# Layer 0 of a two-layer recurrent block: seven smaller place steps on VectorE, the scores one step later, and the rotation of x and the weights at the last gate product

## The reference, cut to what matters

```python
xn = layernorm(x)
s  = attention(xn)          # layer 0: linear attention, 16 heads of 8; layer 1: another linear form
g  = silu(ffn(xn))          # layer 0: 8 experts of width 352, top 2; layer 1: 160 experts of width 64, top 8
x  = x + s * g
```

```python
probs = sigmoid(x @ router_w.T + expert_bias)
top_w, top_idx = top_k(probs, 8)
top_w = top_w / (top_w.sum(-1) + 1e-9) * 2.5
combine[t, top_idx] = top_w
routed = einsum(silu(einsum(x, w_gate)) * combine, w_down)
```

## Time and profile before

| | before |
|---|---|
| median of 3 runs | 1617.26 us (1605.86 to 1618.96) |
| the profiled execution | 1617.64 us, of which the span from first to last instruction is 1615.5 us |
| PE busy | 1270.6 us, 79% of the span |
| DVE busy | 889.2 us, 55% |
| ACT busy | 553.5 us, 34% |
| POOL busy | 553.7 us, 34% |
| mean granted TensorE clock | 0.875 |

### The profile page before, as it was taken

The page is one execution under the profiler, slowest core; times in us unless marked ns, Lnnn a source line. Parts: engine busy times, 40 slices in busy tenths (PEclk is TensorE's granted clock), DMA queues, the critical chain, the costliest instruction groups (busy, mean ns, idle before and its releaser), DMA issues. The chain is left out here.

```text
span 1615.5 us, 20441 instructions
## 1 busy us (share of the span) xinstructions
PE 1270.6 (79%) x6336; PEld 704.5 (44%) x6336; DVE 889.2 (55%) x2575; ACT 553.5 (34%) x1170; POOL 553.7 (34%) x574
## 2 busy tenths in 40 slices
PE   3699988988888898889799891179978777877762
PEld 2334333333333333333333331056966656776652
DVE  3345575675665664665765757600054685486561
ACT  1232322322312322312322220157856355545620
POOL 0000043042052052052061162600065666656565
PEclk9589998998998987998999995579989988898975
DMA  8920020210210210210210213168744444444331
GB/s 270 338 98 1 25 80 27 69 41 22 79 36 17 79 36 17 79 34 18 72 41 12 79 46 119 46 219 255 223 134 121 131 137 131 136 132 138 97 90 42
DMA packets 123235, 152.07 MB, mean 94 GB/s; under 512 B 15277, under 2 KB 82413, under 8 KB 122374
## 3 DMA queue, kind: packets, MB, share of 16 engines
q1 hardware_dynamic: 106758, 117.36, 22.5%
q0 software_dynamic: 16384, 33.59, 7.4%
HBM read 73.30 MB, written 77.60 MB: 93 GB/s over the span
## 5 line engine op out<-in xcount | busy, mean ns | idle before, releaser
L1097 POOL DMA_INDIRECT y<-y_rows,idxy x256 | 269.5, 1053 | 283.7 <-DMA y_rows<-ys 136.8
L1064 POOL DMA_INDIRECT rows<-xn,idx x256 | 252.1, 985 | 83.9 <-issue 82.2
L935 ACT ACTIVATE hs<-GY 128x512 f32<-128x512 f32 x176 | 105.3, 598 | 377.6 <-PE GY L695 306.6
L711 PE MATMUL ACC<-hs,wff 128*128 128x512 f32 x352 | 200.7, 661 | 0.0
L695 PE MATMUL GY<-xn0T,wff 128*128 128x512 f32 x352 | 189.2, 620 | 0.0
L1038 POOL TENSOR_TENSOR rs<-rs,neg_half 128x4 f32<-128x4 f32 x16 | 16.4, 1024 | 453.1 <-DVE rs L1135 453.1
L701 PE MATMUL B<-xw,wff 128*128 128x512 f32 (+2 forms) x272 | 122.6, 630 | 40.9 <-DVE hs L1428 40.9
L1500 DVE SCALAR_TENSOR_TENSOR pos<-neg,pos 128x1024 f32<-128x1024 f32 x8 | 9.8, 1231 | 262.3 <-issue 192.3
L1428 DVE TENSOR_TENSOR hs<-hs,B 128x512 f32<-128x512 f32 x96 | 65.8, 686 | 128.6 <-PE B L701 65.7
L1242 DVE TENSOR_TENSOR att<-X,causal 128x512 f32<-128x512 f32 x128 | 82.6, 686 | 87.7 <-PE X L583 50.7
L842 PE MATMUL X<-y,ident 128*128 128x128 f32 x480 | 78.0, 329 | 64.1 <-DVE y L1587 60.5
(11 more groups left out here) (274 smaller groups left out, 2180.7 us busy)
## 6 DMA issues: line engine op xcount, KB each, us to landing
xg<-rows SPq DMA_DIRECT2D x104, 256.0 KB
y_rows<-ys SPq DMA_DIRECT2D x104, 256.0 KB
rows<-zero SPq DMA_DIRECT2D x7, 2048.0 KB, 9.5
rows<-zero SPq DMA_DIRECT2D x1, 12288.0 KB, 53.9
wff<-in_wgz SPq DMA_DIRECT2D x2, 3840.0 KB, 38.4
wd<-in_wd SPq DMA_DIRECT2D x1, 5120.0 KB, 24.8
wff<-in_w SPq DMA_DIRECT2D x3, 1408.0 KB, 9.2
rows<-xn,idx POOLq DMA_INDIRECT x256
```

Source lines behind the costliest of these rows:

```text
L711: nc.tensor.matmul(ACC[:, :], w2_0[:, v, :], hs[:, v % RH, :], start=(v == 0), stop=(v == U0 - 1))\
L935: nc.scalar.activation(hs[:, u % RH, :], G[u % 2][:, :], ACT.Silu).then_inc(sem["silu_ready"], 1)
L1064: pool.indirect_dma_start(rows, bass.IndirectOffsetOnAxis(ap=idx[:, t * 8 + k:t * 8 + k + 1], axis=0), xn1[:, t, :], None)\
L1097: pool.indirect_dma_start(y8[:, i % RG, k, :], None, y_d[0:groups * Q * P, :], bass.IndirectOffsetOnAxis(ap=idxy[:, b, t * 8 + k:t * 8 + k ...
```

## The change

The table `STEPS` is rewritten. The three reciprocal instructions of `topk1b` become a step of their own, `topk1c`, in slot 20, after `exp0`. The place work is cut into `place_a` to `place_f`, in slots 22, 25, 27, 31, 35 and 39, and `table` in slot 44, where before it was three steps in slots 23, 25 and 28. Scatter goes from slot 29 to 40, qkv0 and rope from 30 and 31 (+2t) to 32 and 33, kp, cum, outer, den and states two or three slots later. qk_T goes from 43 + 10t to 45 + 10t, the scores from 46 and 48 to 49 and 51, the masks from 47 and 49 to 50 and 52, av from 51 to 54; cw0_T, oT_copy, wo and s0 two or three slots later. No instruction is added or removed but for waits. The wait for `acc_done` ahead of the rotation's two copies is taken out.

```diff
@@ -136,16 +136,17 @@
 
 STEPS = {0: ["res_silu"], 1: ["res_gate"], 3: ["res_T"], 4: ["res_add"], 6: ["res_norm"], 9: ["xn1_T", "res_r1"],
          10: ["xn1T_copy"], 11: ["norm0a"], 12: ["router1"], 13: ["probs1"], 14: ["norm0b"], 15: ["topk1a"],
-         16: ["xn0_T"], 17: ["xn0T_copy"], 18: ["topk1b", "router0"], 19: ["exp0"], 21: ["rank"], 48: ["topk0a"], 61: ["topk0b"],
-         23: ["place_a"], 25: ["place_b"], 28: ["place_c"], 29: ["scatter"], 38: ["kp"], 39: ["cum", "outer"], 40: ["den_a"],
-         41: ["states", "den_b"], 72: ["cw0_T", "cw0T_copy"], 82: ["oT_copy"], 84: ["wo"], 85: ["s0"]}
+         16: ["xn0_T"], 17: ["xn0T_copy"], 18: ["topk1b", "router0"], 19: ["exp0"], 20: ["topk1c"], 21: ["rank"],
+         22: ["place_a"], 25: ["place_b"], 27: ["place_c"], 31: ["place_d"], 35: ["place_e"], 39: ["place_f"], 40: ["scatter", "kp"],
+         41: ["cum", "outer"], 42: ["den_a"], 43: ["states", "den_b"], 44: ["table"], 50: ["topk0a"], 62: ["topk0b"],
+         75: ["cw0_T", "cw0T_copy"], 85: ["oT_copy"], 86: ["wo"], 87: ["s0"]}
 for t in range(T):
-    for at, name in ((30 + 2 * t, "qkv0"), (31 + 2 * t, "rope"), (43 + 10 * t, "qk_T"), (44 + 10 * t, "qkT_copy"),
-                     (46 + 10 * t, "scores_a"), (47 + 10 * t, "mask_a"), (48 + 10 * t, "scores_b"), (49 + 10 * t, "mask_b"),
-                     (51 + 10 * t, "av"), (45 + 10 * t, "weights_a"), (50 + 10 * t, "weights_b")):
+    for at, name in ((32 + 2 * t, "qkv0"), (33 + 2 * t, "rope"), (45 + 10 * t, "qk_T"), (46 + 10 * t, "qkT_copy"),
+                     (49 + 10 * t, "scores_a"), (50 + 10 * t, "mask_a"), (51 + 10 * t, "scores_b"), (52 + 10 * t, "mask_b"),
+                     (54 + 10 * t, "av"), (47 + 10 * t, "weights_a"), (54 + 10 * t, "weights_b")):
         STEPS.setdefault(at, []).append((name, t))
 RES = {"res_silu", "res_gate", "res_T", "res_add", "res_norm", "res_r1", "xn1_T", "xn1T_copy", "router1", "probs1",
-       "topk1a", "topk1b", "rank", "place_a", "place_b", "place_c", "weights_a", "weights_b", "scatter"}
+       "topk1a", "topk1b", "topk1c", "rank", "place_a", "place_b", "place_c", "place_d", "place_e", "place_f", "table", "weights_a", "weights_b", "scatter"}
 
 GZ = E1 // 2 * 3 * INTER
 
@@ -1300,6 +1301,9 @@
                 link(nc.vector.tensor_reduce(s8[:], m8[:], AX.X, ALU.add))
                 join()
                 nc.vector.tensor_tensor(chosen, pr2, pr, ALU.not_equal).then_inc(sem["chosen_ready"], 1)
+
+            def s_topk1c(t):
+                join()
                 link(nc.vector.tensor_scalar(s8[:], s8[:], 1e-9, None, ALU.add))
                 join()
                 link(nc.vector.reciprocal(s8[:], s8[:]))
@@ -1318,6 +1322,8 @@
                 link(nc.vector.tensor_scalar(pagesi[:], pagesi[:], 7, None, ALU.arith_shift_right))
                 join()
                 link(nc.vector.tensor_copy(pagesn[:], pagesi[:]))
+
+            def s_place_b(t):
                 join()
                 link(nc.vector.tensor_tensor(new[:], pagesn[:], pages[:], ALU.subtract))
                 link(nc.vector.tensor_copy(hj[:, 0:1], given[:, E1 - 1:E1]))
@@ -1330,21 +1336,27 @@
                 join()
                 link(nc.vector.tensor_tensor(dshift[:], shift[:], shiftn[:], ALU.subtract))
                 link(nc.vector.scalar_tensor_tensor(base[:], shiftn[:], float(P), run[:], ALU.mult, ALU.add))
-                join()
-
-            def s_place_b(t):
-
+
+            def s_place_c(t):
+
+                join()
                 link(nc.vector.scalar_tensor_tensor(shift[:], new[:], 0.0, dshift[:], ALU.is_equal, ALU.mult))
                 link(nc.vector.tensor_scalar(scr[:], dshift[:], float(P), None, ALU.mult))
                 for i, bank in enumerate((X0, X1)):
                     link(nc.vector.tensor_tensor(pr2[:, 2 * i:2 * i + 2, :], bank[:, 0:2 * E1].rearrange("p (t e) -> p t e", t=2),
                                                  limit[:].unsqueeze(1).broadcast_to([P, 2, E1]), ALU.is_le))
+
+            def s_place_d(t):
+
                 join()
                 link(nc.vector.tensor_tensor(shift[:], shift[:], shiftn[:], ALU.add))
                 link(nc.vector.tensor_tensor(pr2, pr2, scr[:].unsqueeze(1).broadcast_to([P, T, E1]), ALU.mult))
                 for i, (bank, done_) in enumerate(((X0, "ranka_read"), (X1, "rankb_read"))):
                     nc.vector.tensor_tensor(place[:, 2 * i:2 * i + 2, :], bank[:, 0:2 * E1].rearrange("p (t e) -> p t e", t=2),
                                             base[:].unsqueeze(1).broadcast_to([P, 2, E1]), ALU.add).then_inc(sem[done_], 1)
+
+            def s_place_e(t):
+
                 dve.wait_ge(*seen.next("ranka_read"))
                 dve.wait_ge(*seen.next("rankb_read"))
                 join()
@@ -1355,7 +1367,7 @@
                 dve.wait_ge(*seen.next("chosen_ready"))
                 nc.vector.tensor_tensor(place, place, chosen, ALU.mult).then_inc(sem["places_ready"], 1)
 
-            def s_place_c(t):
+            def s_place_f(t):
                 dve.wait_ge(*seen.next("places_ready"))
                 nc.vector.memset(pause[:], 0.0)
                 for t in range(T):
@@ -1372,6 +1384,8 @@
                 nc.vector.scalar_tensor_tensor(idx[:], pos_q[:], 1.0 - P, pos_r[:], ALU.mult, ALU.add).then_inc(sem["idx_ready"], 1)
                 link(nc.vector.scalar_tensor_tensor(idxy[:, batch[0], :], pos_q[:], 1.0 - P, pos_r[:], ALU.mult, ALU.add))
 
+            def s_table(t):
+                join()
                 for k in range(JB):
                     link(nc.vector.tensor_scalar(scr[:], given[:], jcol[:, k:k + 1], 0.0, ALU.is_le, ALU.add, accum_out=cj[:, k:k + 1]))
                     join()
@@ -1409,7 +1423,6 @@
 
                     dve.wait_ge(*seen.next("xn0T_ready"))
                     dve.wait_ge(*seen.next("cw0T_ready"))
-                    settled(dve, seen, "acc_done")
                     link(nc.vector.tensor_copy(cw0T[:], cw0Tn[:]))
                     nc.vector.tensor_copy(xn0T[:], xn0Tn[:]).then_inc(sem["rot_ready"], 1)
                 def scaled(e):
```

## The result

| | before | after |
|---|---|---|
| median of 17 runs, same chip | 1610.5 us (1594.94 to 1620.94) | 1597.2 us (1586.94 to 1606.33) |
| ratio, 95% interval | | 0.994 [0.9912, 0.9968] |
| profiled execution / its span | 1617.64 / 1615.5 us | 1586.94 / 1584.8 us |
| mean granted TensorE clock | 0.875 | 0.896 |

The change brought 10 to 13 us where 28 were forecast. The time is inside the range and in the class "within 1%" (0.22), not in the likeliest one. The two profiled executions are 31 us apart and the medians 13: before's lies near the top of what its 17 runs took, after's is the shortest of its 17. So the traces show well which wait went where, and poorly what the sum is worth.

What follows compares the result with a forecast made beforehand. Stage 1 was taken as bound by PE's queue, its idle time and half clock. Terms -25 + 10 - 1.6 - 7.5 - 9.6 - 8 + 14 = -28 took 1617.64 to 1590 us, range 1562 to 1609.

Steps and rivals of the forecast that it cites:

- within 1%: Outcome class for the whole kernel: time within 1%, 16 us, of the kernel before; chance 0.22.
- Part 1: Place work split: PE's wait before unit 7's up product shrinks, new waits come; -25 us in six batches, clock +10.
- Part 2: Last batch with units, f0(7): idx and scatter come later, final res_norm waits for the scatter; only -1.6 us arrive.
- Part 3: Rotation at each batch's start: copies run during down products, PE's waits vanish; -7.5 us (0 to -7.5).
- Part 4: Scores one slot later: PE's wait for ACT's qm shrinks from 4.92 to 3.3 us; -9.6 us, half clock -8.
- Part 5: New slots put topk0b ahead of the second tile's mask_b: av waits 1.4 us, third tile 0.6; +14 us in seven batches.
- I assume this stall stays: Before the second tile's scores: ACT's late silu 13, after 11.35 us idle that no queue ends, was taken as unchanged.
- Rival B: Little arrives: clock falls in all six batches, Part 4 gives nothing, sum 0; with half of Part 4 about 1612 us; chance 0.2.

Runs made afterwards that it cites:

- rotation alone: The kernel before with only the wait for acc_done ahead of the rotation's copies taken out: 1602.44 us, ratio 1.0019; again on another chip 1544.21 us, 0.9986.
- scores back: The changed kernel with scores, masks, av and weights_b one slot earlier again: 1525.91 us, 0.9864, and 1529.56 us, 0.9892, to the kernel before on two chips.
- top-k behind: The changed kernel with topk0a in slot 53 and topk0b in slot 63, behind their tiles' masks: 1530.71 us, ratio 0.9891 to the kernel before.
- scores_back_3: The changed kernel with scores, masks, av and weights_b one slot earlier, where ACT is late: 1600.86 us, 0.9987 to the kernel before; changed kernel beside it 1594.89 us.

## Why the prediction was too large, by its own steps

Where ACT is in time the parts can be told apart. The seven batches take 733.1 us (before, chip B), 729.0 (rotation alone), 712.3 (scores back, on B and on C), 714.0 (top-k behind) and 726.6 (changed). One batch of it, f0(4), in starts of gate products from the batch's first:

| us | unit 8 | unit 12 | unit 16 | unit 19 | end |
|---|---|---|---|---|---|
| before, chip B | 37.7 | 56.9 | 75.8 | 89.1 | 106.1 |
| changed, chip A | 29.3 | 53.4 | 72.7 | 89.2 | 105.7 |
| scores back, chip C | 29.3 | 51.9 | 72.0 | 85.5 | 102.2 |

- **Part 1, net -15: right, -17** (733.1 to 712.3, less 4.1 for the rotation). Unit 8 comes 8.4 us earlier (8.2 forecast), the new waits are 0.9, 0.2 and 2.6, and the half clock after the last is 3.4 us in four of the six batches.
- **Part 2, -1.6: wrong in sign, +5.** From the last rotation to layer 1's first product the trace has 126.0 us before (chip B) and 130.9 after (chip A). The wait for the scatter was seen, but idx is 5.4 us later, not 3.7, and PE's gain ahead of it, which was counted in part, can't be kept at all.
- **Part 3, -7.5: too large.** -4 in the trace, -2 [-5, +1] timed. It left out what DVE waits for next, though the bounds held zero.
- **Part 4, -17.6: true of a late ACT only.** Where ACT is in time it brings nothing (712.3 against 714.0: it costs 1.7). Where it is late it brings about what was said or more: the wait for qm is 9.8 us shorter on chip E, and Parts 4 and 5 together bring some 10 us there, where -17.6 and +14 make 4.
- **Part 5, +14: right.** 726.6 less 712.3 is 14.3, of which 12.6 go with the slots of top-k. Timed, the slots of top-k alone are worth 18.

So without late ACT, by the traces: -17 + 5 - 4 + 0 + 14 = -2; measured 1.0007 +- 0.0025, 1 us.

**The step that failed.** On the result's chip ACT was late, as the prediction had seen, and -10 to -13 us came where -28 were said. Chip E, where ACT is late too, splits this. Parts 4 and 5 did better there than forecast. Parts 1 to 3, which is scores_back_3, brought 2 us [-8, +4] in place of 24. Where ACT is in time the same kernel brings 17 to 21. So the step that failed is "I assume this stall stays": it let Parts 1 to 3 be added in full beside a stall whose price was taken to be the same in both kernels, less only what Part 4 takes from it. Its price moved. By medians (E less A, B or C) late starts cost the kernel before 61 to 62 us, the one with Parts 1 to 3 alone 71 to 75, and the whole change 46. The traces show of what it is made: in the seven batches of the kernel before PE is idle 31 us more and the granted clock is 0.92 in place of 0.97; with Parts 1 to 3 alone PE is idle 41 us more, and the clock is 0.94 in place of 0.99. The timed runs carry this, not the single traces: in those Parts 1 to 3 shorten the seven batches with a late ACT by 17 us too (803.2 and 803.5 to 786.5), but both traces of the kernel before are of long executions, 7 and 13 us above their medians. Part 2, off by 7 us, and Part 3, off by 4 to 6, fall short with ACT in time as well, but they explain the smaller piece of the gap, from 24 to the 17 to 21. That the total still lay within the range owes something to Parts 4 and 5, which made up some 6 us of it.

Why the price of the stall rose is not shown. One reason was looked for, that the scatter now lies beside the steps which make qkT and qm: it begins 45.2 us after the rotation of f0(1), not 36.2 (230.04 - 184.8 against 219.37 - 183.2). ACT's late starts did move to those steps, but they add up to about as much as before (46 us in one trace with Parts 1 to 3 alone, 34 to 41 before), and single traces differ by 10 to 15 us in this sum, so that is too little to settle it. Of the scatter's queue the prediction's Part 2 says that nothing stands behind it; that is true and is no proof that moving it is free. Rival B (little arrives, 1612) was near in size, but by another way: the clock did not fall in all six batches (in five of them, for 3.4 us), and Part 4 gave what it had said.

Still open: what in the scatter delays ACT (single DMAs or unbroken runs of them), through what, and why on some chips only. That the same instruction of ACT's queue is late in batch after batch is a lead which no run followed.

## What to carry to other kernels

An idle time that no queue of the kernel ends is first to be split: what comes before the end of its input is an ordinary wait, and only the rest is late. That rest is to be priced twice, at what the trace shows and at zero, and gains elsewhere in the same batch are not added to it as if it stood still. A label that names no releaser says nothing about lateness by itself. When steps are cut into slots, it is the order inside one slot that decides: two table entries moved by one to three slots (top-k behind the masks, place_f behind the tile's kp) were worth 1% each where ACT is in time, as much as the whole change where it is late. And a profiled execution is one draw: before summing against it, see where it lies among the timed runs.

## What the runs showed of the hardware

- The same program takes 1545.2 to 1545.8 us on three chips, 1602.3 and 1606.9 on two others, and 1610.5 on that of the result. In the traces of the kernel before, 70 us of it lie in the seven batches (803.2 and 803.5 us against 733.1); what follows them differs by at most 6. Without 192 of GpSimd's indirect DMAs the changed kernel takes 726.3 us for the seven batches on one of the slower chips, as on a faster one with them (726.6).
- On those chips ACT starts an instruction up to 9 us after the end of the matmul that it waits for, beside these DMAs and with no semaphore of the kernel in it. DVE can be late too: in f0(1) of the kernel before, unit 13's hs product starts 2.0 us after the end of the silu that it reads. On the others no silu and no copy of q and k in stage 1 is over 1 us late.
- Where an iteration of the program's loop follows another, at f0(4), f0(5) and f0(6), DVE stands 2.3 to 2.6 us before its first instruction with nothing shown to hold it. It does not at f0(1) to f0(3) and f0(7), nor does the profile name a cause.
